# Spreading a group's four indirect gathers over a VectorE turn in a graph-attention edge walk

## The chip, the cores and the metric

The kernel runs on one core of one Trainium2 chip. The metric is the device time of one execution in microseconds. Before the change three runs gave a median of 4069.05 us (4067.04 to 4070.93). The profiled execution, from which all the rows here come, is a separate and slower one: its span is 5874.6 us.

## What is computed

Two layers over a graph of 6,250 nodes with 256 features each. The change touches only the first, an attention layer over 200,000 edges that are sorted by their destination node:

```python
logits  = einsum('ehd,ehd->eh', q[dst], k[src]) / sqrt(D)     # 8 heads of 32
seg_max = segment_max(logits, dst)
expv    = exp(logits - seg_max[dst])
denom   = segment_sum(expv, dst)
agg     = segment_sum((expv / denom[dst])[:, :, None] * v[src], dst)
```

Before it come a layer norm and the projections q, k, v and skip; behind it an update of the nodes, and then a second layer: a small attention that routes (131,072 edges), four experts, and a mix of them by gates.

## The kernel before, in words

The work is done in five stages, one after the other:

1. `prepare` projects the nodes, stores k and v side by side as rows of 520 float32 numbers in `kv_d`, stores q in `q3_d`, and builds tables for the walk.
2. `attend` is the edge walk, which the change touches.
3. `node_update`.
4. `route_experts`, the second layer's edges beside the experts' matmuls. It has indirect gathers of its own (L1389), which the change leaves alone.
5. `route_gates`, which also writes the output.

The walk cuts the edges into 391 groups (`NG`) of four tiles (`G`) of 128 edges, and the nodes into 49 windows of 128. A turn (a step `s`) joins one group with one window. Where a window ends within a group, the group gets a second turn with the next window, so there are 391 + 48 = 439 turns. The program is written out as one body per engine and turn, and each engine works several turns ahead of or behind the others.

What VectorE does in the body of turn `s`, in this order: `tile_maxima(s)` (L807), `segment_max(s+1)` (L796), `scan(s+2)` (L803), `raise_max(s)` (L816, counts `m_new`), `message(s-1)` (L839, counts `msg`), `scale_sums(s-1)` (L834), `fall(s)` (L821), `product(s+4)` (L847, counts `prod`), `logits(s+4)` (L851, counts `lg`), `keep_max(s)` (L825). The body runs 443 times with a product in it, four of them ahead of the first turn. The product multiplies the gathered k rows with the queries `Q` that TensorE spread over the edges (L966); the message multiplies the gathered v rows with the weights, and TensorE sums the messages into `agg_ps` (L1013).

GpSimd (POOL) does one thing in the walk: it fetches the k and v rows. Each `indirect_dma_start` (L746) gathers 128 rows by `src_i` from `kv_d` into one tile of the ring `KV`. That is 128 x 520 x 4 bytes = 266,240 bytes. The ring holds eight groups (`KVR`). Group `n` takes the place of group `n-8`, so POOL first reads from `last_tab` after which turn that group is done with (`end`), and waits until VectorE has counted that many messages (L743). The pair `wait_ge` and `sem_inc` on the next line is one instruction of POOL's sequencer: a wait that updates a semaphore (L744 in the trace). Behind the four gathers of group `n` stands `landed(n-1)` (L736 and L737, one such instruction too): POOL waits until the four gathers of the group before have landed and then adds four to `tiles`, which the products wait for. So a group is told to VectorE only once the next group's four gathers have been handed out.

SyncE fetches each turn's window of q (L760) and its row of resets (L762) seven turns ahead.

Of the kernel before, what the change touches and what calls it, by code (L numbers as in the profile page):

```python
# [36 lines left out]
G = 4  # L37
# [9 lines left out]
KVR = 8  # L47
# [615 lines left out]
def attend(nc, k):  # L663
# [8 lines left out]
    with ExitStack() as ctx:  # L672
# [9 lines left out]
        prod = sb("prod", [P, G, D], F32)  # L682
        lg = [sb(f"lg{i}", [P, TG], F32) for i in range(LOOP)]
# [3 lines left out]
        m_new = [sb(f"m_new{i}", [P, HEADS], BF16) for i in range(2)]  # L687
# [3 lines left out]
        KV = sb("KV", [P, KVR * G, KVW], F32)  # L691
# [11 lines left out]
        ok = {n: nc.alloc_semaphore(f"at_{n}") for n in names}  # L703
# [28 lines left out]
        with nc.Block() as block:  # L732
            @block.gpsimd
            def _(pool):
                def landed(n):
                    pool.wait_ge(kv_landed[n % 4], 16 * G * (n // 4 + 1))  # L736
                    pool.sem_inc(ok["tiles"], G)  # L737

                for n in range(NG):
                    if n >= KVR:  # L740
                        old = n - KVR
                        end = pool.value_load(k.last_tab[0:1, old:old + 1], min_val=1, max_val=RUN)
                        pool.wait_ge(ok["msg"], end)  # L743
                        pool.sem_inc(ok["used"], 1)  # L744
                    for t in range(n * G, (n + 1) * G):
                        pool.indirect_dma_start(out=KV[:, t % (KVR * G), :], out_offset=None, in_=k.kv_d,  # L746
                                                in_offset=bass.IndirectOffsetOnAxis(ap=k.src_i[:, t:t + 1], axis=0)
                                                ).then_inc(kv_landed[n % 4], 16)
                    if n:
                        landed(n - 1)  # L750
                landed(NG - 1)

            @block.sync
# [1091 lines left out]
```

## Time and profile before

| | before |
|---|---|
| median of 3 runs | 4069.05 us (4067.04 to 4070.93) |
| the profiled execution's span | 5874.6 us |
| busy in the profile: PE, DVE, ACT, POOL | 3912.2, 3464.7, 2543.2, 2589.4 us |
| gathers of the walk (L746) | 1564 |
| gathers of the second layer (L1389) | 1024 |

The page gives the span and the busy time of each engine. A group of instructions is shown with its line, engine, operation and tiles, the count, the busy time, the mean of one in ns, and the idle time just before. A timeline gives start and duration in us of each instruction, and in brackets how long its engine had been idle and what ended that. PE is TensorE, DVE is VectorE, ACT is ScalarE, POOL is GpSimd. POOLq is POOL's sequencer, which reads the instructions, waits for semaphores and hands the work on.

### The profile page before, as it was taken

The page shows a single profiled execution, that of the slowest core. Times are in us where ns is not written, and L with a number is a line of the kernel's source. Part 1 is how long each engine was busy: PE and PEld are TensorE (multiplying, and loading weights), DVE is VectorE, ACT ScalarE, POOL GpSimd, SP SyncE. Part 2 cuts the span into 40 slices and gives each one's busy share as a digit, 9 for nine tenths or more (in the row PEclk, how much of TensorE's full clock was granted, in tenths as well). Part 3 has the DMA queues.
Part 4 walks back from the last instruction along what each step waited for, and adds up shares of the span by engine and source line. Part 5 has one row for each costly group of instructions (what it writes and reads, how often), then busy time and mean ns, then how long its engine had stood idle before and what let it go on. Part 6 is the DMA issues. An engine that isn't in the chain of part 4 may idle for free. (4 is left out here: it accounts for less than half of the span.)

```text
span 5874.6 us, 106076 instructions
## 1 busy us (share of the span) xinstructions
PE 3912.2 (67%) x26108; PEld 2753.9 (47%) x26109; DVE 3464.7 (59%) x9273; ACT 2543.2 (43%) x6305; POOL 2589.4 (44%) x2723
## 2 busy tenths in 40 slices
PE   7857777777777777777777773355666666666550
PEld 3335555555555556555555563233434343443330
DVE  8856666666666666666666668434444444444348
ACT  4445555555555555554555555223333333333320
POOL 3244444444444444444445441444444444445540
PEclk9978888888888888888888885577877787777765
DMA  6455555555555555555556555111111111111117
GB/s 212 147 163 165 155 168 163 163 161 168 156 159 163 161 168 156 165 158 165 154 166 172 159 150 177 44 15 18 21 19 21 19 21 19 22 18 19 20 21 263
DMA packets 367690, 683.50 MB, mean 116 GB/s; under 512 B 70294, under 2 KB 240482, under 8 KB 367074
## 3 DMA queue, kind: packets, MB, share of 16 engines
q0 software_dynamic: 157888, 427.05, 27.9%
q1 hardware_dynamic: 183106, 223.68, 11.5%
q10 hardware_dynamic: 26080, 25.70, 1.5%
q8 instruction: 246, 4.03, 0.3%
q14 instruction: 370, 3.03, 0.2%
HBM read 588.41 MB, written 87.78 MB: 115 GB/s over the span
## 5 line engine op out<-in xcount | busy, mean ns | idle before, releaser
L746 POOL DMA_INDIRECT KV<-kv_d,src_i x1564 | 1482.7, 948 | 1677.7 <-DVE msg L839 1232.4
L1389 POOL DMA_INDIRECT re_src<-src_tab_d,rsrc x1024 | 974.5, 952 | 978.7 <-SPq L1399 675.7
L1013 PE MATMUL agg_ps<-msg,oh 128*128 128x264 f32 x3512 | 1085.8, 455 | 229.7 <-issue 218.4
L1013 PEld LDWEIGHTS agg_ps<-msg,oh 128*128 128x128 f32 x3512 | 744.4, 222 | 414.2 <-issue 282.7
L1597 PE MATMUL ex_y_ps<-ex_w,ex_hid 128*112 128x256 f32 x1792 | 586.6, 461 | 301.6 <-issue 299.1
L966 PE MATMUL Q<-q,ohT 128*128 128x256 bf16 x5328 | 753.0, 297 | 15.6 <-issue 13.9
L839 DVE TENSOR_TENSOR msg<-KV,weigh_ps 128x1056 f32<-128x1056 f32 x439 | 545.7, 1243 | 268.6 <-ACT weigh_ps L920 250.1
L1516 ACT COPY re_ohT<-re_ohT_ps 128x1024 bf16<-128x1024 bf16 x179 | 181.0, 1011 | 1075.0 <-remote 1010.6
L966 PEld LDWEIGHTS Q<-q,ohT 128*128 128x128 bf16 x5328 | 531.4, 105 | 117.4 <-issue 19.5
L909 ACT ACTIVATE square<-iota_b,off 128x128 bf16<-128x128 bf16 x1784 | 569.2, 392 | 0.3
L1597 PEld LDWEIGHTS ex_y_ps<-ex_w,ex_hid 128*112 128x112 f32 x1792 | 363.7, 214 | 434.1 <-issue 366.0
L847 DVE TENSOR_TENSOR prod<-KV,Q 128x1024 f32<-128x1024 f32 x443 | 536.1, 1210 | 46.3 <-remote 29.0
L851 DVE TENSOR_REDUCE lg<-prod 128x32 f32<-128x1024 f32 x443 | 540.5, 1220 | 15.1
L897 ACT COPY acc<-agg_ps 128x264 f32 x439 | 166.8, 380 | 701.5 <-remote 400.5
L1585 PE MATMUL ex_h<-acc,ex_w 128*128 (+1 forms) x896 | 446.0, 623 | 20.3 <-issue 16.3
L834 DVE TENSOR_TENSOR agg_ps<-agg_ps,fac 128x264 f32<-128x264 f32 x439 | 190.1, 433 | 405.2 <-issue 263.1
L1466 DVE TENSOR_TENSOR ex_y<-ex_y_ps,ex_b 112x256 f32<-112x256 f32 x224 | 89.9, 418 | 543.3 <-PE ex_y_ps L1597 344.6
L920 ACT ACTIVATE weigh_ps<-weigh_ps 128x32 f32<-128x32 f32 x439 | 80.0, 182 | 648.8 <-remote 560.7
L956 PE MATMUL ohT_ps<-ident_b,oh 128*128 128x128 bf16 x1784 | 208.1, 236 | 198.8 <-issue 170.7
L912 ACT ACTIVATE oh<-square,one 128x512 bf16<-128x512 bf16 x446 | 321.9, 722 | 14.5
L916 ACT COPY ohT<-ohT_ps 128x512 bf16<-128x512 bf16 x445 | 252.3, 567 | 162.5 <-remote 143.2
L807 DVE TENSOR_REDUCE tile_max<-turned_ps 128x8 f32<-128x32 f32 x439 | 83.7, 191 | 380.0 <-remote 377.3
(264 smaller groups left out, 6199.0 us busy)
## 6 DMA issues: line engine op xcount, KB each, us to landing
q<-q_d SPq DMA_DIRECT2D x446, 192.0 KB
y_d<-ex_y ACTq DMA_DIRECT2D x56, 448.0 KB
rg_ye<-y_d SPq DMA_DIRECT2D x7, 3584.0 KB, 11.8
KV<-kv_d,src_i POOLq DMA_INDIRECT x1564
nu_xs<-xs_d SPq DMA_DIRECT2D x7, 2688.0 KB, 11.9
re_src<-src_tab_d,rsrc POOLq DMA_INDIRECT x1024
kv_d<-pr_kv SPq DMA_DIRECT2D x49, 260.0 KB, 2.2
xs_d<-pr_xs SPq DMA_DIRECT2D x49, 256.0 KB, 2.4
```

What stands on the lines that cost most here:

```text
L746: pool.indirect_dma_start(out=KV[:, t % (KVR * G), :], out_offset=None, in_=k.kv_d, in_offset=bass.IndirectOffsetOnAxis(ap=k.src_i[:, t:t ...
L839: v.tensor_tensor(m[:, :, :, :], KV[:, tiles(s), D:KVW].rearrange("p t (h e) -> p t h e", e=HW), bc(p_ps.rearrange("p (t h) -> p t h", h=H ...
L847: v.tensor_tensor(prod[:, :, :], KV[:, tiles(s), 0:D], Q[ring(s, 2)][:, :, :], ALU.mult).then_inc(ok["prod"], 1)
L851: v.reduce_sum(lg[s.slot][:, :], prod[:, :, :].rearrange("p t (h d) -> p (t h) d", d=DH), AX.X).then_inc(ok["lg"], 1)
L909: q = act.activation(square[:, t, :], k.iota_b[:, :], ACT.Square, bias=off[s.slot][:, t:t + 1])
L912: act.activation(oh[ring(s, OHR)][:, :, :], square[:, :, :], ACT.Relu, bias=k.one[:, :], scale=-1.0).then_inc(ok["oh"], 1)
L916: act.copy(ohT[ring(s, OHR)][:, :, :], ohT_ps[:, :, :]).then_inc(ok["ohT"], 1)
L966: m = pe.matmul(Q[ring(s, 2)][:, t, :], ohT[ring(s, OHR)][:, t, :], q3[s.slot][:, c * D:(c + 1) * D], start=(c == 0), stop=(c == 2))
L1013: m = pe.matmul(agg_ps[:, 0:HEADS * HW], oh32[ring(s, 2)][:, t, :], msg[ring(s, 2)][:, t, :, :].rearrange("p h e -> p (h e)"), start=False ...
L1389: pool.indirect_dma_start(out=gs[:, t % (RING * RG), :], out_offset=None, in_=k.src_tab_d, in_offset=bass.IndirectOffsetOnAxis(ap=k.rsrc[: ...
L1585: m = pe.matmul(h_ps[f % 2][:, 0:UN], k.w1_sb[:, u.at % NE, c, f * P:(f + 1) * P], k.xT[:, bass.ds(u.block, 1), c, half * UN:(half + 1) * ...
L1597: m = pe.matmul(y_ps[w % 2][0:YN, 0:D], hid[u.at % 2][:, f, w * YN:(w + 1) * YN], k.w2_sb[:, u.at % NE, f, :], start=(f == 0), stop=(f == ...
```

## The change

Group `n` from the ninth on still waits for the messages of group `n-8` before its first gather. The second gather now waits in addition until VectorE has counted `end + 5` products, the third until it has counted `end + 5` logits, the fourth until it has counted `end + 2` new maxima. Each wait comes with a `sem_inc` on `used`. And `landed(n-1)` no longer stands behind the fourth gather of group `n`, but behind its second: for all groups but the first, those of the first eight too. The tiles, the rows that are gathered, and the ring are as before.

```diff
             def _(pool):
+                PACE = (("prod", 5), ("lg", 5), ("m_new", 2))
+
                 def landed(n):
                     pool.wait_ge(kv_landed[n % 4], 16 * G * (n // 4 + 1))
                     pool.sem_inc(ok["tiles"], G)
@@
                         end = pool.value_load(k.last_tab[0:1, old:old + 1], min_val=1, max_val=RUN)
                         pool.wait_ge(ok["msg"], end)
                         pool.sem_inc(ok["used"], 1)
-                    for t in range(n * G, (n + 1) * G):
-                        pool.indirect_dma_start(out=KV[:, t % (KVR * G), :], out_offset=None, in_=k.kv_d,
-                                                in_offset=bass.IndirectOffsetOnAxis(ap=k.src_i[:, t:t + 1], axis=0)
+                    for t in range(G):
+                        if n >= KVR and t:
+                            paced, ahead = PACE[t - 1]
+                            pool.wait_ge(ok[paced], end + ahead)
+                            pool.sem_inc(ok["used"], 1)
+                        pool.indirect_dma_start(out=KV[:, (n * G + t) % (KVR * G), :], out_offset=None, in_=k.kv_d,
+                                                in_offset=bass.IndirectOffsetOnAxis(ap=k.src_i[:, n * G + t:n * G + t + 1], axis=0)
                                                 ).then_inc(kv_landed[n % 4], 16)
-                    if n:
-                        landed(n - 1)
+                        if n and t == 1:
+                            landed(n - 1)
                 landed(NG - 1)
```

## Rows read from the trace of the kernel before

**Rows 1.** The page: the span and its instructions

```profile
span 5874.6 us, 106076 instructions
```

**Rows 2.** The span cut at the stages: busy us of each engine, clock, DMA share

```profile
0.00:340.00 340.00, 271.50 (x761) 115.08 (x762) 289.45 (x497) 149.18 (x459) 100.88 (x127) 0.94 0.50 174
340.00:3543.00 3203.00, 2375.53 (x18103) 1830.25 (x18101) 2076.18 (x4401) 1661.96 (x4878) 1482.39 (x1564) 0.85 0.56 161
3543.00:3740.00 197.00, 70.32 (x305) 63.30 (x305) 152.00 (x349) 98.68 (x165) 31.40 (x9) 0.53 0.47 159
3740.00:5740.00 2000.00, 1194.89 (x6943) 745.28 (x6941) 837.38 (x3775) 629.73 (x799) 974.77 (x1025) 0.76 0.13 19
5740.00:5875.00 135.00, 0.00 (x0) 0.00 (x0) 109.71 (x253) 3.63 (x5) 0.00 (x0) 0.50 0.78 286
```

**Rows 3.** The products of all turns: duration min/median/max, first and last start

```profile
L847 DVE TENSOR_TENSOR prod<-KV,Q x443: 1200/1214/1222, 353.5 to 3536.5; 128x1024 f32<-128x1024 f32 x148
```

**Rows 4.** What VectorE waited for in the walk: us, times, longest

```profile
DVE tile_max L807 <- remote: 377.3, 98, 5.6
DVE agg_ps L834 <- issue: 263.1, 85, 6.7
DVE msg L839 <- ACT weigh_ps L920: 250.1, 135, 6.2
DVE agg_ps L834 <- ACT acc L897: 141.9, 95, 8.1
DVE prod L847 <- remote: 29.0, 1, 29.0
```

**Rows 5.** VectorE's timeline near the walk's end: starts of three products

```profile
3527.25 1.22 DVE L847 TENSOR_TENSOR prod<-KV,Q 128x1024 f32<-128x1024 f32 x1
...
3531.87 1.20 DVE L847 TENSOR_TENSOR prod<-KV,Q 128x1024 f32<-128x1024 f32 x1
...
3536.47 1.21 DVE L847 TENSOR_TENSOR prod<-KV,Q 128x1024 f32<-128x1024 f32 x1
```

**Rows 6.** The gathers of both layers: duration min/median/max, first and last start

```profile
L746 POOL DMA_INDIRECT KV<-kv_d,src_i x1564: 943/949/1296, 339.6 to 3494.4; - x196
...
L1389 POOL DMA_INDIRECT re_src<-src_tab_d,rsrc x1024: 942/947/1330, 3740.4 to 5692.5; - x171
```

**Rows 7.** What POOL waited for before the walk's gathers

```profile
POOL KV L746 <- DVE msg L839: 1232.4, 240, 21.7
...
POOL KV L746 <- issue: 438.1, 1315, 8.5
```

**Rows 8.** POOL's timeline: two groups of four gathers, back to back

```profile
3402.03 0.95 POOL L746 DMA_INDIRECT KV<-kv_d,src_i  x1 [3.57 <-DVE msg L839]
3403.29 0.95 POOL L746 DMA_INDIRECT KV<-kv_d,src_i  x1 [0.30 <-issue]
...
3405.79 0.95 POOL L746 DMA_INDIRECT KV<-kv_d,src_i  x1 [0.30 <-issue]
...
3409.56 0.95 POOL L746 DMA_INDIRECT KV<-kv_d,src_i  x1 [0.31 <-issue]
```

**Rows 9.** Instruction `landed` (L737) at 3402 to 3415 us: first and last start

```profile
L737 POOLq EVENT_SEMAPHORE  x2: 17/17/17, 3403.2 to 3409.6; - x2
```

**Rows 10.** The message that ended before the gather at 3402.03

```profile
3399.99 1.25 DVE L839 TENSOR_TENSOR msg<-KV,weigh_ps 128x1056 f32<-128x1056 f32 x1 [2.28 <-ACT weigh_ps L920]
```

**Rows 11.** The walk's last two groups' fourth gathers, and `landed` (L737) at 3490 to 3499

```profile
3489.35 0.94 POOL L746 DMA_INDIRECT KV<-kv_d,src_i  x1 [0.30 <-issue]
...
3494.35 0.94 POOL L746 DMA_INDIRECT KV<-kv_d,src_i  x1 [0.30 <-issue]
...
L737 POOLq EVENT_SEMAPHORE  x2: 17/17/17, 3493.6 to 3498.5; - x2
```

**Rows 12.** Another fourth gather, and `landed` (L737) at 521 to 530

```profile
522.62 0.95 POOL L746 DMA_INDIRECT KV<-kv_d,src_i  x1 [0.30 <-issue]
...
L737 POOLq EVENT_SEMAPHORE  x1: 17/17/17, 526.4 to 526.4; - x1
```

**Rows 13.** All messages: duration min/median/max

```profile
L839 DVE TENSOR_TENSOR msg<-KV,weigh_ps x439: 1233/1235/1256, 399.5 to 3539.4; 128x1056 f32<-128x1056 f32 x147
```

## The prediction

> **What bounds the kernel now.** The profiled execution spans 5874.6 us [rows 1], 1.44 times the median of 4069.05 us of the runs, so its time can't be taken as it stands. I first cut it by stage [rows 2]: 340 us ahead of the walk's first gather, 3203 us of walk, 197, 2000 and 135 us for the three stages behind it. In the walk no engine is busy throughout; VectorE has 2076 of 3203 us. Then I asked what VectorE waits for there [rows 4]: things that hang on TensorE and on ScalarE behind it, together some 1030 us, and hardly ever for a product's input; its one long wait there, 29 us, is at the start. The reader is to see in VectorE's timeline [rows 5] that when those waits are absent, products start 4.60 and 4.62 us apart. That is a turn at VectorE's own pace. I call it 4.61 us.
>
> The second engine that matters is POOL. Its gather takes 0.95 us with 0.30 us ahead of it [rows 8]: from 3402.03 to 3409.56 us six gathers follow one another in 7.53 us, 1.255 us each. Four of them are 5.02 us, more than a turn. Only because 391 groups share 439 turns does POOL keep up: 391 x 5.02 = 1963 us against 439 x 4.61 = 2024 us. POOL is 97% full when VectorE runs at its own pace. The profile hides this, for there the mean turn is (3536.5 - 353.5) / 442 = 7.20 us [rows 3], and POOL waits 1232 us for messages [rows 7].
>
> Is a plain run really at 4.61 us? I add the stages up, each at its own pace. To the end of the walk: 339.6 to the first gather [rows 6], 13.9 to the first product [rows 3], 442 x 4.61 = 2037.6, and 6.3 from the last product (3536.5 us) to the cut at 3543 [rows 2]: 2397 us. Then 197. Then the second layer at POOL's pace, 1024 x 1.255 = 1285, and 47.5 from its last gather [rows 6] to the cut at 5740 us. Then 135. The sum is 4062 us, 0.2% below the median. So I read a plain run as one without the profile's extra TensorE stalls: VectorE bounds the walk, POOL's gathers bound the second layer. This was one profiled execution, and I make the sum for the change against this 4062 us and carry the difference over to the median.
>
> **The change, part by part.** POOL's sequencer is not the same thing as POOL. The instruction `landed` at 3403.2 us [rows 9] stands in the code behind a group's fourth gather, yet it passes before the second of that group's gathers starts at 3403.29; the fourth starts at 3405.79 [rows 8]. So the sequencer hands out four gathers ahead of the engine, and a wait behind the fourth gather holds up nothing, as long as it is over soon.
>
> *The moved `landed`.* This is the costly edit. In steady back-to-back work the sequencer really does sit in it: the fourth gather of a group starts at 3405.79 us and its `landed` passes at 3409.6, 3.8 us later [rows 8, 9]; 522.62 and 526.4 make 3.8 too [rows 12]; 3489.35 and 3493.6 make 4.25, 3494.35 and 3498.5 make 4.15 [rows 11]. That is the time from a gather's start to the moment POOL may count on its data. Before, the next four gathers were already handed out, and they cover 5.02 us, so it costs nothing. After, only two are, which cover until 3 x 1.255 = 3.77 us after the old group's fourth start, and the third gather must moreover be dispatched anew. What a dispatch takes is seen where a message frees POOL: the message ends at 3399.99 + 1.25 = 3401.24, the gather starts at 3402.03 [rows 10, 8], 0.79 us later. Behind `landed` stands one more semaphore instruction (the wait for logits); each shows as 17 ns, and I put 0.05 us for it and its reading. So the third gather starts 3.75 + 0.05 + 0.79 = 4.59 us after the previous group's fourth, instead of 3.77. The fourth follows 1.25 us later. A group's cycle becomes 4.59 + 1.25 = 5.84 us. For the landing I take 3.75, just below the 3.8 of the two ordinary rows, since the fourth gather will be only the second of its burst, with fewer transfers queued ahead; the ends are 3.4 (an estimate, as far below as the slow rows lie above) and 4.15.
>
> 5.84 us is more than the 439 / 391 x 4.61 = 5.18 us per group that VectorE allows, so POOL becomes the bound and its lag adds up until VectorE waits in the product for `tiles`. The last group's fourth gather starts at 339.6 + 390 x 5.84 + 5.0 = 2622 us; 3.75 to land; then about four turns and the last message and sums, 4 x 4.61 + 6.3 = 24.7. The walk ends at 2651 us instead of 2397: **+253 us**. The slack that the ring gives (two or three turns) is used up in the first two or three windows and changes the start of the waiting, not this sum, since POOL runs without a break from its first gather.
>
> *The three new waits.* With the message of turn `end` at hand, the product that makes `end + 5` comes in the same body, the logits right behind, the maxima early in the next body. In VectorE's own pace the fourth could go one turn (4.61 us) minus a message after the first: about 3.4 us, where POOL itself needs 3.76. A POOL that runs late finds all three satisfied. They cost three sequencer instructions of 17 ns, hidden under a gather, and nothing on the path: 0 us. If that cover failed, 0.1 us per gather would be 391 x 0.3 = 117 us, but only where dispatch bounds, and there two of the three waits lie off the chain that I priced.
>
> *What it may bring.* The spreading can help only if bursts slow something. Products last 1.200 to 1.222 us and messages 1.233 to 1.256 [rows 3, 13] with gathers in flight or not, so VectorE gains nothing. Earlier `tiles` help nobody: VectorE's waits for products in the walk are 29 us, at the start [rows 4]. I take 0, with 15 us as the most.
>
> *Weighed against a rule.* The rows say 3.8 to 4.25 us from a gather's start to its landing. The Trainium skill, "DMA: Bandwidth & Descriptors", section "Anatomy of one DMA — SWDGE (gpsimd) path", fits one such DMA as 2.0 us plus bytes over 436 GB/s. By that an estimate for 266,240 bytes is 2.6 us, the cycle would be 4.7 us, and the change would cost nothing. The rows here contradict that figure by over a microsecond.
>
> **The rivals.**
> (a) *No change*: in a run without recording, the data lands sooner. The point from which it decides is a landing of 5.18 - 1.25 - 0.84 = 3.09 us; below it POOL keeps up and the time is 4069 us. For it: recording slows the profiled run in other places. Against it: POOL's cadence from the profile adds up to the right time of plain runs, and no row here shows under 3.8.
> (b) *Faster*: in plain runs the bursts of four hold up the fetches of q (seven turns ahead) or SyncE's queue, and the spread frees them. Against it: the product waits only at the start [rows 4]. At most the 15 us: 4055 us. It needs a landing under 3.09 too.
> (c) *Slower, by less*: VectorE is not alone; TensorE holds a plain turn nearer 4.85 us and the other stages are shorter than in the profile. Then the walk before is 442 x 0.24 = 106 us longer, POOL's bound is unchanged, and the cost is 147 us: 4216 us. The stages' sum leaves room for some of it only.
> (d) *Slower, by more*: the landing is like the slow rows, 4.15 us [rows 11]. The cycle is 6.24, another 391 x 0.4 = 156 us: 4478 us.
> (e) *The change doesn't spread*: that is part of my forecast, not apart from it. The gathers will not follow VectorE's four marks but go two and two, split by the landing.
>
> **How the numbers follow.** My forecast, +253 us on 4069, is 4322 us, with its own range 4240 to 4400 and a chance of 0.56. (c) gets 0.18, (d) 0.11, (a) 0.09, (b) 0.06. A landing of 3.4 gives 4322 - 391 x 0.35 = 4185 us, and lies with (c). The range from 4130 to 4430 holds the forecast, (c) and the lower part of (d), and leaves out (a), (b) and the rest of (d), some 2 in 10. A change of 0.2% (8 us) is about what a measurement of this kernel can tell from none. Faster: 0.06, same: 0.09, slower: 0.85.
>
> **What would show it.** In the changed profile: the third gather of a group starts about 4.6 us after the fourth of the group before when POOL is behind, with some 0.8 us of idle ahead of it put down to the KV transfer; `landed` stands ahead of each third gather; the first eight groups, before any pacing, already go at 5.84 us per group. The profile's span may hardly move (its turns of 7.2 us leave 8.1 us for a group), while the runs do. It is wrong if POOL keeps 1.25 us between second and third gather, or if the landing falls under 3.1 us.

## The result and the profile after

The changed kernel takes 4345.41 us (median of 4 runs, 4342.48 to 4348.65) beside 4068.07 us before: ratio 1.0681, 95% interval 1.0666 to 1.0696, slower by 277 us. Forecast were 4322 us and a range of 4130 to 4430.

The profile of the changed kernel spans 4343.9 us, as long as a plain run. The first profile of the kernel before, from which the forecast was made, spans 5874.6 us [rows 1]. I therefore compare with a second profile of the kernel before, of 4066.1 us (the first experiment below). The span cut at the stages, the kernel before (second profile); columns as in [rows 2]:

```profile
0.00:340.00 340.00, 270.06 (x759) 114.69 (x760) 288.50 (x496) 148.80 (x458) 100.66 (x126) 0.94 0.50 174
340.00:2424.00 2084.00, 1992.60 (x18101) 1628.91 (x18102) 2029.40 (x4402) 1628.37 (x4878) 1479.34 (x1564) 0.99 0.82 248
2424.00:2622.00 198.00, 70.95 (x307) 63.87 (x306) 152.02 (x349) 98.56 (x165) 31.46 (x9) 0.56 0.47 158
2622.00:3932.00 1310.00, 1004.34 (x6943) 646.37 (x6941) 844.77 (x3778) 640.34 (x799) 985.94 (x1025) 0.92 0.18 29
```

The changed kernel:

```profile
0.00:340.00 340.00, 270.25 (x760) 114.91 (x761) 288.56 (x497) 148.53 (x458) 100.64 (x126) 0.94 0.50 174
340.00:2704.00 2364.00, 2029.31 (x18103) 1655.32 (x18103) 2062.02 (x4402) 1684.71 (x4879) 1478.07 (x1564) 0.97 0.74 219
2704.00:2901.00 197.00, 70.21 (x304) 63.44 (x305) 151.93 (x349) 98.62 (x165) 31.23 (x9) 0.53 0.47 159
2901.00:4210.00 1309.00, 999.65 (x6943) 643.90 (x6941) 845.81 (x3781) 640.04 (x799) 984.59 (x1025) 0.93 0.18 29
```

The walk grew from 2084 to 2364 us, by 280; the other stages agree within 1 us. In the walk VectorE was busy 2029 of 2084 us before (97%) and has about the same work in a longer time now. The gathers, first of the second profile before, then of the changed kernel (durations, first and last start):

```profile
L746 POOL DMA_INDIRECT KV<-kv_d,src_i x1564: 940/946/1295, 340.4 to 2385.4; - x196
```

```profile
L752 POOL DMA_INDIRECT KV<-kv_d,src_i x1564: 940/946/1295, 340.2 to 2673.3; - x196
```

A gather takes as long as ever. From the first group's fourth gather (4.1 us after the first start) to the last's are 390 groups: (2385.4 - 340.4 - 4.1) / 390 = 5.23 us per group before, (2673.3 - 340.2 - 4.1) / 390 = 5.97 us after. Below, "cycle" is this number.

POOL's timeline of the changed kernel shows where 0.74 us a group go; it answers to [rows 8]. The gather at 2004.53 is the third of its group:

```profile
2002.58 0.95 POOL L752 DMA_INDIRECT KV<-kv_d,src_i  x1 [0.30 <-issue]
2004.53 0.94 POOL L752 DMA_INDIRECT KV<-kv_d,src_i  x1 [1.01 <-DMA KV<-kv_d,src_i]
2005.78 0.95 POOL L752 DMA_INDIRECT KV<-kv_d,src_i  x1 [0.31 <-issue]
2007.03 0.95 POOL L752 DMA_INDIRECT KV<-kv_d,src_i  x1 [0.30 <-issue]
2008.29 0.95 POOL L752 DMA_INDIRECT KV<-kv_d,src_i  x1 [0.30 <-issue]
2010.21 0.94 POOL L752 DMA_INDIRECT KV<-kv_d,src_i  x1 [0.98 <-DMA KV<-kv_d,src_i]
```

Third and fourth gather, then the next group's first and second, go 1.25 us apart; then POOL is idle for a microsecond, and what ends it is the landing of the gathers. The `landed` instruction (L739 here) in the same stretch, as in [rows 9] a line with the count and the first and last start, for a window that ends at 2010 us:

```profile
L739 POOLq EVENT_SEMAPHORE  x2: 17/17/17, 2003.7 to 2009.4; - x2
```

The fourth gather starts at 2005.78, `landed` passes at 2009.4 (3.6 us later), the next group's third gather starts at 2010.21 (0.8 us later). Over all groups of this trace, `landed` passes 3.86 us behind the start of the fourth gather in the mean and 3.70 in the median, and the third gather starts 0.86 us behind `landed` in the mean, 0.85 in the median.

The first eight groups have none of the three new waits, and they are as slow: the fourth gather of the first group starts at 344.35 us and that of the eighth at 386.21, and 41.86 / 7 = 5.98 us a group.

And what POOL and VectorE waited for in the changed kernel; the second line of POOL's is the usual 0.3 us between gathers:

```profile
POOL KV L752 <- DMA KV<-kv_d,src_i: 407.1, 337, 3.6
POOL KV L752 <- issue: 369.1, 1151, 2.0
POOL KV L752 <- DVE m_new L822: 54.8, 32, 2.3
```

```profile
DVE prod L853 <- POOLq L739: 214.2, 197, 9.3
DVE prod L853 <- PE Q L972: 42.0, 46, 2.5
```

VectorE's new wait is the product's, and POOL's sequencer ends it with `landed`. The row with `m_new` looks like pacing. But all 32 of its gaps stand before a group's third gather, and the wait for the maxima is that of the fourth; in the groups that I followed the maxima had been there for some 10 us. The profile names the last event that it has where the landing's own is missing, so these gaps belong to `landed` too.

### The profile page after: what moved, and what is told of

Same layout as the page of the kernel before. It is cut to its first block and busy times, and to the rows that moved or that the text cites. A ratio compares the mean times of both kernels' runs of the same rounds, so it can differ in the third digit from the quotient of the medians.

```text
span 4343.9 us, 107991 instructions
## 1 busy us (share of the span) xinstructions
PE 3369.4 (78%) x26108; PEld 2477.6 (57%) x26109; DVE 3457.4 (80%) x9273; ACT 2575.5 (59%) x6305; POOL 2594.5 (60%) x2723
## 5 line engine op out<-in xcount | busy, mean ns | idle before, releaser
L1019 PE MATMUL agg_ps<-msg,oh 128*128 128x264 f32 x3512 | 910.4, 404 | 1.6 <-DVE agg_ps L840 1.6
L1019 PEld LDWEIGHTS agg_ps<-msg,oh 128*128 128x128 f32 x3512 | 647.3, 194 | 92.2 <-ACT oh L929 1.7
L972 PE MATMUL Q<-q,ohT 128*128 128x256 bf16 x5328 | 678.9, 279 | 1.3
L1603 PE MATMUL ex_y_ps<-ex_w,ex_hid 128*112 128x256 f32 x1792 | 441.6, 390 | 0.0
L981 PE MATMUL turned_ps<-ident,lg 128*32 128x128 f32 x442 | 119.8, 271 | 326.0 <-DVE running L809 320.1
L1603 PEld LDWEIGHTS ex_y_ps<-ex_w,ex_hid 128*112 128x112 f32 x1792 | 303.2, 179 | 53.8
L929 ACT CAST oh<-oh 128x512 f32<-128x512 bf16 x439 | 272.8, 621 | 0.0
L1428 DVE TENSOR_SCALAR re_oh<-iota_b,re_off 128x128 bf16<-128x128 bf16 x1432 | 255.3, 278 | 11.6 <-issue 4.3
L981 PEld LDWEIGHTS turned_ps<-ident,lg 128*32 128x32 f32 x442 | 41.6, 94 | 385.6 <-DVE lg L857 318.5
L1565 PE MATMUL re_ohT_ps<-ident_b,re_oh 128*128 128x128 bf16 x1432 | 119.2, 231 | 174.9 <-DVE re_oh L1428 170.1
```

The costliest lines, as they stand in the source:

```text
L929: act.copy(oh32[ring(s, 2)][:, :, :], oh[ring(s, OHR)][:, :, :]).then_inc(ok["oh32"], 1)
L972: m = pe.matmul(Q[ring(s, 2)][:, t, :], ohT[ring(s, OHR)][:, t, :], q3[s.slot][:, c * D:(c + 1) * D], start=(c == 0), stop=(c == 2))
L1019: m = pe.matmul(agg_ps[:, 0:HEADS * HW], oh32[ring(s, 2)][:, t, :], msg[ring(s, 2)][:, t, :, :].rearrange("p h e -> p (h e)"), start=False ...
L1603: m = pe.matmul(y_ps[w % 2][0:YN, 0:D], hid[u.at % 2][:, f, w * YN:(w + 1) * YN], k.w2_sb[:, u.at % NE, f, :], start=(f == 0), stop=(f == ...
```

## The experiments

Theory A is the forecast's: the landing wait behind the second gather makes POOL the bound. Theory B blames the three new waits, C both. D and E are other forms of A's cost. F and G come up further down: F is about the price of a satisfied wait, G about what makes some landings late.

**The kernel before, profiled again.** No edit.

> The kernel before, once more, for a profile beside that of the change. The changed kernel's profile spans 4343.9 us, as its plain runs do, while the first profile of the kernel before spans 5874.6 us against 4068 us of its runs. If the long TensorE waits of that first profile belong to that one execution, this one spans about 4066 us, the products of the walk are 4.6 us apart in the mean, POOL's gathers 1.25 us apart, and the walk ends near 2397 us. If they belong to any recording of this kernel, it spans about 5870 us again.

It took 4067.92 us, its profile 4066.1 us. Its products run from 349.2 to 2418.0 us:

```profile
L847 DVE TENSOR_TENSOR prod<-KV,Q x443: 1200/1201/1222, 349.2 to 2418.0; 128x1024 f32<-128x1024 f32 x148
```

That is 2068.8 / 442 = 4.68 us a turn, where the first profile had 7.20 [rows 3] and its best turns 4.6 [rows 5]. The walk ends at 2424 us, not at 2397. The long TensorE waits of the first profile did not come back. TensorE's granted clock in the walk is 0.99 here and was 0.85 there, and the same instructions kept it busy for 1993 us here and 2376 there [rows 2]. That is 383 of the 1119 us by which that walk was longer; what the rest came from isn't shown.

What VectorE waits for in this walk comes to some 37 us in all, 16.6 of them in five waits for a group to land:

```profile
DVE prod L847 <- POOLq L737: 16.6, 5, 8.8
```

TensorE is busy for 1993 of the 2084 us, and its largest wait is for VectorE's scan (67 us in all). So VectorE bounds the plain walk, with TensorE close behind.

**The three waits alone.**

```diff
-                        if n and t == 1:
-                            landed(n - 1)
+                    if n:
+                        landed(n - 1)
```

> The three new waits stay, the landing wait goes back behind the fourth gather. Theory A (the moved landing wait costs it all): no change, 4068 us, within 8 us. Theory B (the waits for product, logits and maxima hold POOL back): about 4345 us. Theory C (both, in parts; the changed profile names new maxima before 55 us of POOL's idle time): about 4125 us.

4068.72 us, ratio 1.0001 (0.9992 to 1.0010). POOL's rows now name maxima (27.6 us, 66 times), logits (21.6, 71) and products (17.0, 54), but for logits and products that is no more than 0.3 us each, the usual step between two gathers, and for maxima little more. The starts of the gathers tell how much the waits hold back. Of the 383 groups that have them, 54 start the second gather more than 0.1 us late (14 in the kernel before), none the third and 3 the fourth (0 and 0 before). From a group's first gather to its fourth it is 3.86 us in the mean, where it was 3.79. So these waits hardly spread the gathers, and nowhere near over a turn of 4.68 us. A stretch of this kernel, with one second gather held back for 0.3 us more than usual:

```profile
1001.09 0.95 POOL L752 DMA_INDIRECT KV<-kv_d,src_i  x1 [1.60 <-DVE msg L845]
1002.64 0.94 POOL L752 DMA_INDIRECT KV<-kv_d,src_i  x1 [0.60 <-issue]
1003.89 0.94 POOL L752 DMA_INDIRECT KV<-kv_d,src_i  x1 [0.31 <-DVE m_new L822]
1005.14 0.95 POOL L752 DMA_INDIRECT KV<-kv_d,src_i  x1 [0.30 <-DVE msg L845]
```

The last gather starts at 2387.9 us, 2045.1 after the first, as without the waits (2045.0). The pacing by itself neither costs nor gains. B falls.

**The moved landing wait alone.**

```diff
-                        if n >= KVR and t:
-                            paced, ahead = PACE[t - 1]
-                            pool.wait_ge(ok[paced], end + ahead)
-                            pool.sem_inc(ok["used"], 1)
```

> The landing wait stands behind the second gather as in the change, the three new waits are gone. Theory A: about 4345 us, a cycle of 5.97 us per group. Theory B: 4068 us. Theory C: about 4290 us.

4317.77 us, ratio 1.0612 (1.0596 to 1.0629). Some 250 of the 277 us are the moved wait's. 28 us are left, and since the three waits cost nothing in the run before, they come from the two together. Its gathers:

```profile
L748 POOL DMA_INDIRECT KV<-kv_d,src_i x1564: 940/946/1295, 344.7 to 2643.8; - x196
```

The cycle is 5.88 us, 0.09 less than in the changed kernel. There, the wait for the logits stands right behind `landed`, on the path: from `landed` to the third gather it is 0.86 us in the mean there and 0.76 here, and the landings are alike (3.86 and 3.88). 390 x 0.09 = 35 us; in this profile the first gather starts 4.5 us later, which leaves about 30. The run with more such instructions, below, tests this.

**The landing wait one gather later**, behind the third, with the pacing and without it. The second run also leaves out the three waits, as above.

```diff
-                        if n and t == 1:
+                        if n and t == 2:
```

> The change with its landing wait one gather later, behind the third. Theory A: the next gather then starts 3.86 + 0.85 = 4.7 us after the old group's fourth (4.45 to 5.5 with the spread of the landing), where POOL's own pace asks for 5.0 us; so nearly nothing, 4068 to 4085 us. Theory B: 4345 us. Rival D (any wait for a landing within a group costs POOL the sequencer's lead, wherever it stands): 4200 us or more.

> The landing wait behind the third gather without the three new waits. With them it cost 16 us (ratio 1.0044). If these come from the late part of the landings (over 4.3 us, behind which the next gather is late), they stay, less 0.1 us of semaphore instruction in the groups that are late: 4075 to 4085 us beside 4068 us before. If they come from the pacing: 4068 us.

With pacing 4083.49 us, ratio 1.0044 (1.0030 to 1.0057), cycle 5.30 us; without it 4081.97 us beside 4073.17 us of the kernel before in that session, ratio 1.0022 (1.0012 to 1.0033), cycle 5.27. So one gather more in hand removes nearly all of the cost, as A says, and D falls. What stays without the pacing is 9 us. POOL is still named as waiting for landings:

```profile
POOL KV L748 <- DMA KV<-kv_d,src_i: 94.2, 134, 2.8
```

These are late landings. In 133 groups of that trace the fourth gather, the one behind the wait, starts more than 0.1 us late, and in each of them `landed` passed 4.35 us or more behind the old group's fourth gather (4.79 in the mean, 3.95 in the other groups). In the kernel before, no fourth gather is late. The pacing may add about as much again here, but the intervals of the two ratios overlap.

**The landing wait one gather earlier**, behind the first (`t == 0`), without the three waits.

> No pacing; the landing wait stands behind the first gather, so one gather is handed out ahead of it. Theory A (the sequencer waits 3.9 us for the landing, then 0.75 us to the next gather's start, and what is handed out before does not count): the cycle is 3.9 + 0.75 + 2 x 1.25 = 7.15 us per group against 5.23 in the kernel before, 390 x 1.92 = +749 us, about 4815 us. Rival E (the cost of the wait is a fixed one per group, about 0.65 us as in the run with the wait behind the second gather): about 4320 us.

5072.13 us, ratio 1.2450 (1.2431 to 1.2469). E falls, but A's number is 257 us short. POOL's timeline of this kernel, and its `landed` between 2003 and 2017 us:

```profile
2003.55 0.94 POOL L748 DMA_INDIRECT KV<-kv_d,src_i  x1 [2.72 <-DMA KV<-kv_d,src_i]
2004.80 0.95 POOL L748 DMA_INDIRECT KV<-kv_d,src_i  x1 [0.30 <-issue]
2006.05 0.95 POOL L748 DMA_INDIRECT KV<-kv_d,src_i  x1 [0.30 <-issue]
2007.30 0.95 POOL L748 DMA_INDIRECT KV<-kv_d,src_i  x1 [0.30 <-issue]
2011.26 0.94 POOL L748 DMA_INDIRECT KV<-kv_d,src_i  x1 [3.02 <-DMA KV<-kv_d,src_i]
```

```profile
L739 POOLq EVENT_SEMAPHORE  x1: 17/17/17, 2010.5 to 2010.5; - x1
```

The group's fourth gather is now the third of its burst (2006.05), and its landing comes 4.45 us later instead of 3.6; in the mean over all groups it is 4.44 instead of 3.86. The gathers run from 339.3 to 3381.0 us, so the cycle is 7.79 us, and 390 x (7.79 - 5.23) = 998 us: 4075.0 + 998 = 5073. The form of the sum holds (landing + 0.75 + 2 x 1.25 = 7.7); I had taken the landing of a second gather for a third.

**Two groups back.** The wait keeps its place, but asks for the group before last.

```diff
-                        if n and t == 1:
-                            landed(n - 1)
+                        if n > 1 and t == 1:
+                            landed(n - 2)
+                landed(NG - 2)
                 landed(NG - 1)
```

> The change with its three waits and its place of the landing wait, but the group that is waited for is the one before last, whose data landed a group's time earlier. Theory A: the wait passes at once, no cost, 4068 us within 8 us. Rival D (any semaphore wait within a group costs the lead): 4200 us or more.

4075.06 us beside 4075.0, ratio 1.0000 (0.9991 to 1.0009). With the data already there, the same instruction at the same place costs nothing. So it isn't the wait within the group but the time that the sequencer has to sit in it. This is the change with its loss mended; it doesn't beat the kernel before.

**Four more semaphore instructions** behind the landing wait of the changed kernel, all satisfied.

```diff
                         if n and t == 1:
                             landed(n - 1)
+                            for _ in range(4):
+                                pool.wait_ge(kv_landed[(n - 1) % 4], 16 * G * ((n - 1) // 4 + 1))
+                                pool.sem_inc(ok["used"], 1)
```

> The changed kernel with four more semaphore instructions behind the landing wait, all of them satisfied at once. The changed kernel has one such instruction more there than the run with the moved wait alone, and is 28 us slower, its cycle 0.09 us longer. Theory F (each satisfied one on this path costs about 0.09 us per group): 390 x 0.36 = +140 us on the changed kernel, about 4485 us. Rival (they cost their recorded 17 ns): +27 us, about 4372 us; or nothing, 4345 us, if the 28 us came from the pacing itself.

4578.50 us, ratio 1.1234 (1.1217 to 1.1251), more than any theory had. The four in one group, and `landed` ahead of them:

```profile
L739 POOLq EVENT_SEMAPHORE  x1: 17/17/17, 2009.0 to 2009.0; - x1
```

```profile
L759 POOLq EVENT_SEMAPHORE  x4: 17/17/17, 2009.1 to 2009.4; - x4
```

They are recorded as 17 ns and follow one another at 0.1 us; the next gather starts at 2010.27, 1.2 us behind `landed` instead of 0.85. So 0.1 us each is right, and it explains the 28 us above. The cycle grew by 0.59 us, from 5.97 to 6.56. The four account for some 0.4 of it, and the landing for 0.2: it is 4.06 us in the mean, where it was 3.86. Why it became longer is open.

**Less of the q fetch.** Landings of 3.55 and of over 4.3 us both occur. Does the fetch of q get in their way?

A third of it, from the seventh turn on:

```diff
-                    sp.dma_start(q3[s.slot][:, :], k.q3_d[bass.ds(w * P, P), :]).then_inc(window_landed[s.slot], 16)
+                    c = 3 * D if isinstance(s.base, int) and s.v < LOOP else D
+                    sp.dma_start(q3[s.slot][:, 0:c], k.q3_d[bass.ds(w * P, P), 0:c]).then_inc(window_landed[s.slot], 16)
```

Nearly none:

```diff
-                    sp.dma_start(q3[s.slot][:, :], k.q3_d[bass.ds(w * P, P), :]).then_inc(window_landed[s.slot], 16)
+                    if isinstance(s.base, int) and s.v < LOOP:
+                        sp.dma_start(q3[s.slot][:, :], k.q3_d[bass.ds(w * P, P), :]).then_inc(window_landed[s.slot], 16)
+                    else:
+                        sp.dma_start(q3[s.slot][0:16, 0:128], k.q3_d[bass.ds(w * P, 16), 0:128]).then_inc(window_landed[s.slot], 16)
```

> The changed kernel, but from the seventh turn on only the first third of each window of q is fetched (64 instead of 192 KB a turn); the rest of the tile keeps old numbers, so the logits are not those of the reference. It tests why a landing takes 3.55 us in some groups and over 4.3 in others. Theory G (the late ones share the DMA engines with the fetch of q): the mean landing falls from 3.86 to about 3.65 us, the cycle from 5.97 to about 5.76 us, 390 x 0.21 = 82 us less, about 4265 us. Rival (the spread comes from the gathers' own rows): 4345 us.

> The changed kernel, but from the seventh turn on the fetch of q moves 16 rows of 256 bytes (4 KB) instead of 128 rows of 1536 bytes; the logits are again not those of the reference. With a third of the bytes in the same 128 rows the landing stayed at 3.83 us against 3.86. If it is the rows of the fetch and not its bytes that get between the gathers' rows, the mean landing now falls to about 3.65 us, the cycle to 5.76 us and the time by 82 us to about 4265 us. If the fetch of q has nothing to do with it: 4345 us.

4342.83 us, ratio 1.0657 (1.0640 to 1.0673), and 4335.78 us, ratio 1.0640 (1.0623 to 1.0656), against the change's 1.0681 (1.0666 to 1.0696). Their cycles are 5.94 and 5.93 us. So the fetch of q is worth some 0.04 us a group, where theory G asked for 0.21, and it falls. What spreads the landings stays open.

## Why the prediction was right, point by point

**What bounds the kernel before** was read rightly from a profile that was 1.44 times too long: the second profile shows VectorE busy for 97% of the walk, and about 4.61 us is what a turn takes there without the 37 us of waits: (2068.8 - 37) / 442 = 4.60. The stages' sum of 4062 us was right in part by two errors that cancel. With the waits the turn is 4.68 us in the mean, not 4.61, so the walk ends 27 us later; and the second layer takes 1310 us, not 1285 + 47.5 = 1332.

**The lead of the sequencer and the moved wait.** This step carried the forecast, and it held in its form: from the fourth gather to the passing of `landed`, then to the third gather's start, then 1.25 us. The first eight groups, which the forecast named as a sign, went at 5.98 us where it had 5.84, and the idle time ahead of a third gather was about 1.0 us where it had 0.8. Its terms against the measured ones:

| term | forecast | measured |
|---|---|---|
| `landed` to the third gather | 0.84 us | 0.85 us |
| third to fourth gather | 1.25 | 1.25 |
| landing | 3.75 | 5.97 - 2.10 = 3.87 in the mean |
| cycle | 5.84 | 5.97 |
| walk's end, before and after | 2397, 2651 | 2424, 2704 |
| difference | +253 us | +277 us in the runs |

The term that was too small is the landing. I took it from the ordinary rows, and for those it was good: the median is 3.70 us. I allowed nothing for the late ones, which raise the mean, so 390 x 0.13 = 51 us are missing after; before, 27 us are missing by the turn. The difference of the two is the error of the forecast.

The rule that I weighed, 2.0 us plus bytes over 436 GB/s (the Trainium skill, "DMA: Bandwidth & Descriptors", section "Anatomy of one DMA — SWDGE (gpsimd) path"), would have given an estimate of 2.6 us for a landing and no change. Counted from the start of the gather on POOL, as this sum needs it, 3.87 us were measured; taking the row was the right choice, and rival (a) fell with it. Of the 3.87 us POOL itself is busy for the first 0.95, and from there on it is 2.92 us. So over half of the difference may lie in the moment from which one counts.

**The three waits** were forecast at 0 us. By themselves that is right (1.0001). But in the changed kernel the wait for the logits, behind `landed`, costs about 28 us. I had it in the sum at 0.05 us; it is 0.09 to 0.1. The 17 ns of its row are not its price.

**What spreading may bring** was forecast at 0 us. The runs with the waits and without the loss (1.0001 and 1.0000) show that these three waits bring nothing. What gathers that are really spread over a turn would bring isn't shown, for in both runs the time from a group's first gather to its fourth grew by 0.07 us only.

**The rivals.** (a) and (b) are out. (c) supposed a turn of 4.85 us that TensorE holds; it is 4.68, TensorE is busy for 96% of the walk but none of VectorE's waits there names it, and the longer landing more than made up for the slower turn. (d), all landings at 4.15 us, is out, though single ones come that late. (e) held: in the changed kernel the gathers go two and two between landings, and VectorE's four marks hardly matter, neither there nor without the moved wait.

**The profile's span.** I thought that recording slows this kernel and that the span might not move. It is an error without effect on the time: a profile at plain speed was to be had of both.

## What to carry to other kernels

POOL's sequencer worked ahead of POOL here, and this lead is what hid a wait for landed data. Before moving such a wait, count what is already handed out ahead of it and compare it with the landing plus the dispatch, here 3.9 + 0.8 = 4.7 us in the mean. With four gathers of 1.25 us handed out the wait cost nothing, with three (the next starts 5.0 us after the old fourth, at POOL's own pace) 0.2%, with two 6%, with one 24%. Late landings count one by one, so leave room for them and not for the mean alone. Where the wait can ask for data one group older, it passes at once; behind the second gather this took away the whole cost.

## What the runs showed of the hardware that I had not expected

- The landing of a gather isn't one number. The fourth gather of a group took 3.86 us in the mean where it was the second of a burst, and 4.44 us where it was the third (the landing wait behind the first gather). The place isn't all, for with four more semaphore instructions the second of a burst took 4.06 us. Single ones in the changed kernel run from 3.5 to 6.2 us.
- A satisfied semaphore instruction of POOL's sequencer, recorded as 17 ns, takes about 0.1 us on the path to the next gather. Four of them, together with a longer landing that I can't explain, made the kernel 233 us slower than the change.
- One profiled execution of this kernel was 44% longer than its plain runs, at a mean granted clock of 0.81, and the next one not at all, at 0.93 (5874.6 and 4066.1 us).
